# One graph layer and its gate, two blocks merged into one pipelined stage

## What is computed

```python
# layer 0, graph: U = eigenvectors of the normalised Laplacian of adj (64 x 64)
agg = einsum('mn,bnd->bmd', U.T, layernorm(x));  h = relu(agg @ W1 + b1)
x = x + einsum('nm,bmd->bnd', U, h @ W2 + b2)
# layer 0, experts: gate, the best 2 of 8, softmax over these two
z = layernorm(x);  logits = z @ Wg + bg;  top_w, top_i = top_k(logits, 2);  w = softmax(top_w)
x = x + sum over the two experts of w * (gelu(z @ W1[e] + b1[e]) @ W2[e] + b2[e])
# layer 1, graph (two mixings with adj, then LSTMs over windows of nodes), layer 1, experts (best 1 of 8)
```

## Time and profile before

| what | us |
|---|---|
| median of three runs | 1786.4 (1785.47 to 1787.1) |
| the profiled execution | 1787.28, its span 1785.5 |
| busy: PE / DVE / ACT / POOL | 1275.3 / 836.7 / 761.6 / 602.5 |
| first matmul of `layer_gnn0` | at 336.69 |
| first normalize of `gate0` | at 392.66 |
| first DVE instruction of `route` | at 443.90 |

### The profile page before, as it was taken

How to read it: one execution, slowest core, us unless ns; L and a number is a source line. 1 busy time by engine, 2 the same in 40 slices (tenths; PEclk the granted TensorE clock), 3 DMA queues, 4 the chain that set the end, 5 groups by cost and what they waited for, 6 DMA issues and landing times. The chain is left out here.

```text
span 1785.5 us, 26992 instructions
## 1 busy us (share of the span) xinstructions
PE 1275.3 (71%) x6055; PEld 905.0 (51%) x6056; DVE 836.7 (47%) x3364; ACT 761.6 (43%) x1937; POOL 602.5 (34%) x1091
## 2 busy tenths in 40 slices
PE   2444225577679999966777779989885995799900
PEld 1233225467569999963434433444333453799900
DVE  5777999575842222225565523333336336311122
ACT  3555445111555555433344335444445553555400
POOL 4666145000035566547555200000000000355466
PEclk9999656685789999996688779999997997699955
DMA  9200000002002222221111000000000110122333
GB/s 261 63 1 1 1 1 1 1 24 71 0 25 70 71 71 71 66 56 52 37 37 34 20 1 0 0 0 0 0 0 0 42 47 6 24 69 70 61 94 100
DMA packets 87134, 69.13 MB, mean 39 GB/s; under 512 B 11158, under 2 KB 77020, under 8 KB 87068
## 3 DMA queue, kind: packets, MB, share of 16 engines
q1 hardware_dynamic: 73884, 41.40, 8.1%
q0 software_dynamic: 13184, 27.03, 6.3%
HBM read 41.38 MB, written 27.00 MB: 38 GB/s over the span
## 5 line engine op out<-in xcount | busy, mean ns | idle before, releaser
L1250 POOL COPY g_idx<-sitter 128x1 int32 (+1 forms) x78 | 11.9, 179 | 553.7 <-POOLq L1112 538.1
L1657 PE MATMUL ps<-BIG,w_ihT 128*128 x364 | 162.2, 589 | 20.7 <-ACT e_go L1679 15.0
L1304 ACT ACTIVATE c_H<-ps,c_b 128x256 f32<-128x256 f32 x284 | 117.4, 471 | 131.4 <-PE ps L1333 130.6
L1254 POOL DMA_INDIRECT c_Z<-z,c_idx x142 | 138.6, 976 | 81.0 <-POOLq L1252 57.4
L1444 POOL DMA_INDIRECT d_Y<-y,seat x128 | 129.1, 1009 | 94.5 <-DVE X L1458 49.1
L1346 PE MATMUL ps<-w_dn,c_H 128*128 x1136 | 139.0, 276 | 2.1 <-ACT c_H L1304 2.0
L1333 PE MATMUL ps<-c_ZT,c_w 128*128 128x256 f32 x568 | 136.3, 383 | 1.2 <-ACT c_ZT L1292 1.2
L1346 PEld LDWEIGHTS ps<-w_dn,c_H 128*128 128x128 f32 x1136 | 132.4, 192 | 3.5 <-issue 3.0
L1657 PEld LDWEIGHTS ps<-BIG,w_ihT 128*128 128x128 f32 x364 | 69.3, 194 | 108.6 <-issue 108.6
L1663 PE MATMUL ps<-e_hs,w_hhT 128*128 128x512 f32 (+1 forms) x256 | 110.8, 575 | 12.9 <-DVE e_hs L1709 12.9
L1333 PEld LDWEIGHTS ps<-c_ZT,c_w 128*128 128x128 f32 x568 | 103.6, 192 | 13.4 <-ACT c_ZT L1292 2.0
(11 more groups left out here) (495 smaller groups left out, 2951.8 us busy)
## 6 DMA issues: line engine op xcount, KB each, us to landing
y<-c_ys SPq DMA_DIRECT2D x71, 128.0 KB, 1.8
z<-ZB SPq DMA_DIRECT2D x32, 256.0 KB, 2.2
y<-g_ys SPq DMA_DIRECT2D x39, 128.0 KB, 1.8
out_dram<-X SPq DMA_DIRECT2D x32, 128.0 KB, 1.9
c_Z<-z,c_idx POOLq DMA_INDIRECT x142, 2.5
w_up<-in_L_ffn_W_dram SPq DMA_DIRECT2D x1, 2048.0 KB
w_dn<-in_L_ffn_W_dram SPq DMA_DIRECT2D x8, 256.0 KB
w_dn<-in_L_ffn_Wd_dram SPq DMA_DIRECT2D x8, 256.0 KB
```

Of the source, the lines that this page charges most:

```text
L1250: pool.tensor_copy(idx[h][u][:, :], k.sitter[:, ds(t * HALVES + h, 1)]).then_inc(copied, 1)
L1254: pool.indirect_dma_start(Z[u][:, h, :], None, z, bass.IndirectOffsetOnAxis(ap=idx[h][u][:, 0:1], axis=0)).then_inc(fetched[u], 16)
L1304: act.activation(H[u][:, c, :], UP[u][c // 2][:, c % 2 * SLOT_TILE:(c % 2 + 1) * SLOT_TILE], ACT.Gelu, bias=(b1[u] if w_up is not None els ...
L1657: last = pe.matmul(o, k.w_ihT[:, w, :], state(i, u, s, p, wide, lanes), start=True, stop=(s == 0))
```

## The change

`layer_gnn0` and `gate0` are replaced by one block, `layer0`. Turns 0 to 27 run on all engines; the gate's work on group n is done in turn n + 9 (`LAG`).

- The layer's MIX and BACK, and the gate's transposes, have one PSUM bank each instead of two; DN keeps two. DVE's order in a turn is add(g-2), stats(g-3), bias(g-1), and then the chunk work below.
- Mean and 1/std are formed per chunk of four groups (16 tiles): `variance` in turns 6, 10, 14, 18 and `scale` in turns 7, 11, 15, 19, with a Sqrt of ACT between.
- Normalising moves from DVE to POOL (two tiles of a group) and ACT (the other two).
- The gate's scores use the strips of `gate1`: four matmuls of 128 x 32 weights and 128 moving columns, a copy by ACT (`sc`), and one matmul with the identity for all four tiles.
- The picks run per chunk, in DVE turns 15, 19, 23 and 27.
- The softmax's Exp moves to ACT's part of `route`, and its three DVE instructions to the start of `gnn1`.
- One more memset on POOL at the kernel's start, since the gate's weight tile is now 32 columns wide.

```diff
-CONSTS = 11 + E
+CONSTS = 12 + E
...
+                      pool.memset(k.upper[:, :], 0.0), pool.memset(k.w_gate1[:, :, :], 0.0),
+                      pool.memset(k.w_gate0[:, :], 0.0)]
...
-def layer_gnn0(nc, k, sem):
...
-def gate0(nc, k, sem, z):
...
+def layer0(nc, k, sem, z):
+    mixed, h_ready, dn_done, o_ready, back_done, added, s_stats = (
+        sem("a_" + n) for n in "mixed h dn o back added stats".split())
+    s_va, s_root, scaled, z_act, z_pool, turned, turned_sb, scores, scores_sb, logits = (
+        sem("b_" + n) for n in "va root scaled z_act z_pool turned turned_sb scores scores_sb logits".split())
     kept = [sem(f"b_kept{u}") for u in range(2)]
+    MIX, DN, BACK, TR, SC, GA = k.ps[0], k.ps[1:3], k.ps[3], k.ps[4], k.ps[5], k.ps[6:8]
+    CHUNK = 4
+    WIDE = CHUNK * GT
+    LAG = 2 * CHUNK + 1
+    TURNS = GROUPS + LAG + 3
+    zt = rows_of_tiles(z)
     with ExitStack() as own:
+        def mine(name, shape):
+            return own.enter_context(nc.sbuf_tensor(f"a_{name}", shape, F32))
+        O, HT = ([mine(f"{n}{u}", [P, GC]) for u in range(2)] for n in ("O", "H"))
+        sc = [mine(f"sc{u}", [P, P]) for u in range(2)]
+        nbias, m1, m2 = (mine(n, [P, TILES]) for n in ("nbias", "m1", "m2"))
+        tm = mine("tm", [P, WIDE, E])
         block = own.enter_context(nc.Block())
+        def chunk(q):
+            return slice(q * WIDE, (q + 1) * WIDE)
         @block.vector
         def _(dve):
             link = Chain(dve, k.ch)
+            def add_bias(g):
+                dve.wait_ge(dn_done, g + 1)
+                if g >= 2:
+                    dve.wait_ge(back_done, g - 1)
+                dve.tensor_tensor(O[g % 2][:, :].rearrange("p (t d) -> p t d", d=D),
+                                  DN[g % 2][:, :].rearrange("p (t d) -> p t d", d=D),
+                                  k.b_g0dn[:, None, :].to_broadcast([P, GT, D]), ALU.add).then_inc(o_ready, 1)
+            def add_back_tokens(g):
+                dve.wait_ge(back_done, g + 1)
+                dve.tensor_tensor(group_of(k.X, g), group_of(k.X, g),
+                                  BACK[:, :].rearrange("p (t d) -> p t d", d=D), ALU.add).then_inc(added, 1)
+            def variance(q):
+                r = chunk(q)
+                me, ve, mo, vo = (k.st6[:, r, n] for n in (1, 2, 4, 5))
+                dve.wait_ge(s_stats, (q + 1) * CHUNK)
+                got = link.put(dve.tensor_tensor(k.va[:, r], me, mo, ALU.subtract))
+                link.put(dve.tensor_tensor(k.vb[:, r], ve, vo, ALU.add))
+                sums = link.put(dve.tensor_tensor(k.mean[:, r], me, mo, ALU.add))
+                link.need(got)
+                link.put(dve.tensor_tensor(k.va[:, r], k.va[:, r], k.va[:, r], ALU.mult))
+                link.need(sums)
+                link.put(dve.tensor_scalar(k.vb[:, r], k.vb[:, r], 1.0 / D, EPS, ALU.mult, ALU.add))
+                link(dve.tensor_scalar(k.mean[:, r], k.mean[:, r], 0.5, None, ALU.mult))
+                dve.scalar_tensor_tensor(out=k.va[:, r], in0=k.va[:, r], scalar=0.25, in1=k.vb[:, r],
+                                         op0=ALU.mult, op1=ALU.add).then_inc(s_va, 1)
+            def scale(q):
+                r = chunk(q)
+                dve.wait_ge(s_root, q + 1)
+                link(dve.reciprocal(k.vb[:, r], k.rstd[:, r]))
+                link(dve.tensor_tensor(k.vb[:, r], k.vb[:, r], k.va[:, r], ALU.mult))
+                link(dve.tensor_tensor(k.vb[:, r], k.vb[:, r], k.rstd[:, r], ALU.add))
+                link(dve.tensor_scalar(k.vb[:, r], k.vb[:, r], 0.5, None, ALU.mult))
+                link(dve.reciprocal(k.rstd[:, r], k.vb[:, r]))
+                dve.scalar_tensor_tensor(out=nbias[:, r], in0=k.mean[:, r], scalar=-1.0, in1=k.rstd[:, r],
+                                         op0=ALU.mult, op1=ALU.mult).then_inc(scaled, 1)
+            def picks(q):
+                r = chunk(q)
+                dve.wait_ge(logits, (q + 1) * CHUNK)
+                link(dve.tensor_tensor(k.LG[:, r, :], GA[q % 2][:, 0:WIDE * E].rearrange("p (t e) -> p t e", e=E),
+                                       k.b_gate0[:, None, :].to_broadcast([P, WIDE, E]), ALU.add))
+                pick_first(dve, link, k, k.LG[:, r, :], WIDE, k.K1[:, r, :], m1[:, r], tm[:, :, :])
+                link(dve.scalar_tensor_tensor(out=k.LG[:, r, :], in0=k.K1[:, r, :], scalar=-1e30, in1=k.LG[:, r, :],
+                                              op0=ALU.mult, op1=ALU.add))
+                pick_first(dve, link, k, k.LG[:, r, :], WIDE, k.K2[:, r, :], m2[:, r], tm[:, :, :])
+                link(dve.tensor_tensor(k.W2[:, r], m2[:, r], m1[:, r], ALU.subtract))
+            for g in range(TURNS + 2):
+                if 2 <= g < GROUPS + 2:
+                    add_back_tokens(g - 2)
+                if 3 <= g < GROUPS + 3:
+                    dve.wait_ge(added, g - 2)
+                    token_stats(dve, k, g - 3, s_stats)
+                if 1 <= g < GROUPS + 1:
+                    add_bias(g - 1)
+                for q in range(GROUPS // CHUNK):
+                    if g == (q + 1) * CHUNK + 2:
+                        variance(q)
+                    if g == (q + 1) * CHUNK + 3:
+                        scale(q)
+                    if g == (q + 1) * CHUNK + LAG + 2:
+                        picks(q)
             link.reset()
+        @block.gpsimd
+        def _(pool):
+            for n in range(GROUPS):
+                u = n % 2
+                pool.wait_ge(scaled, n // CHUNK + 1)
+                if n >= 2:
+                    pool.wait_ge(turned, n - 1)
+                    pool.wait_ge(kept[u], 16 * (n // 2))
+                for j in range(GT // 2):
+                    t = n * GT + j
+                    last = pool.tensor_scalar(k.ZB[u][:, j * P:(j + 1) * P], k.X[:, t, :], k.mean[:, t:t + 1],
+                                              k.rstd[:, t:t + 1], ALU.subtract, ALU.mult)
+                last.then_inc(z_pool, 1)
         @block.scalar
         def _(act):
+            def normalized(n):
+                u = n % 2
+                act.wait_ge(scaled, n // CHUNK + 1)
+                if n >= 2:
+                    act.wait_ge(turned, n - 1)
+                    act.wait_ge(kept[u], 16 * (n // 2))
+                for j in range(GT // 2, GT):
+                    t = n * GT + j
+                    last = act.activation(k.ZB[u][:, j * P:(j + 1) * P], k.X[:, t, :], ACT.Identity,
+                                          bias=nbias[:, t:t + 1], scale=k.rstd[:, t:t + 1])
+                last.then_inc(z_act, 1)
+            for g in range(TURNS):
+                n = g - LAG
+                for q in range(GROUPS // CHUNK):
+                    if g == (q + 1) * CHUNK + 3:
+                        act.wait_ge(s_va, q + 1)
+                        act.activation(k.rstd[:, chunk(q)], k.va[:, chunk(q)], ACT.Sqrt).then_inc(s_root, 1)
+                if g < GROUPS:
+                    act.wait_ge(mixed, g + 1)
+                    if g >= 2:
+                        act.wait_ge(dn_done, g - 1)
+                    act.activation(HT[g % 2][:, :], MIX[:, :], ACT.Relu, bias=k.b_g0up[:, :]).then_inc(h_ready, 1)
+                if 0 <= n < GROUPS:
+                    act.wait_ge(turned, n + 1)
+                    if n >= 2:
+                        act.wait_ge(scores, n - 1)
+                    act.activation(k.ZS[n % 2][:, :], TR[:, :], ACT.Copy).then_inc(turned_sb, 1)
+                if 1 <= n <= GROUPS:
+                    act.wait_ge(scores, n)
+                    if n >= 3:
+                        act.wait_ge(logits, n - 2)
+                    act.activation(sc[(n - 1) % 2][:, :], SC[:, 0:P], ACT.Copy).then_inc(scores_sb, 1)
+                if 0 <= n + 1 < GROUPS:
+                    normalized(n + 1)
         @block.tensor
         def _(pe):
+            for g in range(TURNS):
+                n = g - LAG
+                if g < GROUPS:
+                    if g >= 1:
+                        pe.wait_ge(h_ready, g)
                     for j in range(GT):
                         c = slice(j * P, (j + 1) * P)
+                        last = pe.matmul(MIX[:, c], k.BIG[:, g * GC + j * P:g * GC + (j + 1) * P], k.BDU[:, :],
+                                         start=True, stop=True)
+                    last.then_inc(mixed, 1)
+                if 2 <= g < GROUPS + 2:
+                    pe.wait_ge(o_ready, g - 1)
+                    if g >= 3:
+                        pe.wait_ge(added, g - 2)
+                    pe.matmul(BACK[:, :], k.BDUT[:, :], O[g % 2][:, :], start=True, stop=True).then_inc(back_done, 1)
+                if 0 <= n < GROUPS:
+                    pe.wait_ge(z_act, n + 1)
+                    pe.wait_ge(z_pool, n + 1)
+                    if n >= 1:
+                        pe.wait_ge(turned_sb, n)
+                    for j in range(GT):
+                        c = slice(j * P, (j + 1) * P)
```

(68 more changed lines are left out.)

108 lines of the change are left out of this document (removed).

## The result

Over 6 runs each the changed kernel takes 1778.8 us in the median (1775.7 to 1782.2), the kernel before 1786.75 (1785.5 to 1791.5): ratio 0.995, 95% interval 0.9933 to 0.9968. The forecast was 1774.2 with a range of 1767 to 1782. The profiled execution took 1782.2 (span 1780.4), 5.1 less than the profiled one of before, so the traces have to explain 5.1 us, the medians 8.

The account below looks back on a forecast made before the run. PE's wasteful half-clock gate work and some 18 us holding one engine only bound the stage; turns, stall, gate and tail summed to `route` 12.2 us earlier, so 1787.3 gives 1775.1, 1774.2 as median; range 1767 to 1782.

Parts of the forecast that it names:

- The layer's turn: Layer turns before the gate joins: a closed loop on in-order DVE of 3.35 us, against 2.80 before.
- Mixed turns: Turns 10 to 15, layer and gate together: PE's own sum of 3.9 us each at full clock.
- slower rival: PE's clock does not hold in the layer's turns, at 84% busy: 34 us more, 1808; chance 0.06.
- The stall: DVE turn 15: `scale(2)` and `picks(0)` delay BACK(15) to 401.3, with some 4.5 us of idle PE.
- The gate alone: Groups 8 to 15 after the layer: a chain through single banks and ACT, 2.9 us a group at half clock.
- first rival: Gate alone near 2.45 us a group, through a higher clock or cheaper `picks(0)`: 3 to 5 us less, 1770; chance 0.15.
- Scale(3) ends some 8 us after BACK(15), before ACT needs it: Gate alone: the last chunk's scales come in time, as ACT needs them in its fourth turn, over 10 us.
- The tail: From the last transposes at 423.4 through the last picks of 4.1 us to the start of `route` at 431.7.
- No overlap, the last rival: Some wait puts the gate behind the layer after all: 109 us for the stage, about 1788; chance 0.02.
- The softmax at nothing: Moved softmax costs nothing: ACT's idle 22.14 us in `route` and DVE's 6.61 us wait in `gnn1` cover it.
- second rival: DVE and POOL block each other while POOL normalises: 5 us more, 1779; chance 0.12.
- The total: Whole kernel: `route` begins 12.2 us earlier, taking the profiled 1787.3 to 1775.1, or 1774.2 for the median.

Follow-up runs that it names:

- e_stats_last: Changed kernel with DVE's bias ahead of the statistics in each turn: stage 93.4 us, ratio 0.9923 to the kernel before.
- e_choose_late: Changed kernel with the first chunk's choosing (twelve operations of its picks) moved to turn 20: stage 88.9 us, ratio 0.9911 to the kernel before.
- e_scale_first: Changed kernel with the chunks' scales ahead of the picks within a turn: stage 94.1 us, one time of 1816.7 us.
- e_lag17: Changed kernel with the gate's work lagging 17 turns instead of 9: stage 108.1 us, ratio 1.002 to the kernel before.
- e_pad: Changed kernel with 17 dummy DVE operations at the end of the merged stage: stage 108.0 us, ratio 1.0006 to the kernel before.
- e_again: Changed kernel run again on other cores, no edit: stage 96.1 us, median 1818.3 us, ratio 0.9958 to the kernel before.
- e_before_again: The kernel before run again on other cores, no edit: stage 106.4 us, median 1824.0 us.
- e_old_scores: Changed kernel with scores computed as in the kernel before, without strips, `sc` copy and identity matmul: stage 94.4 us, ratio 0.9919.
- e_three: Changed kernel with bias before statistics, scales ahead of picks and the first chunk's choosing in turn 20: stage 85.9 us, ratio 0.9907.

## Why the prediction was right, point by point

The mechanisms of the stage held, one by one, but that its sum fits to 0.1 us is in part luck. Up to BACK(15) the stage gained 1.1 us on the forecast, the gate alone lost 0.7 of it and the tail 0.3.

- **The layer's turn**: forecast 3.35, measured 3.28, and `e_stats_last` shows that DVE's loop is the cause. Turn 10's BACK was put at 370.75 and came at 370.44. Chunk work in turns 6 and 7 cost nothing, as forecast: the seven turns are 3.27 or 3.28.
- **Mixed turns**: forecast 3.9, measured 3.86 for the row above. Its parts by starts are transposes 0.53 (forecast 0.45), strips 0.36 (0.45) and identity matmul 0.14 (0.2). The reading that strips run beside each other holds at 128 columns: in series at the rate of the earlier trace rows they would be 0.89. The clock held at 1.00 in the layer's turns, which the slower rival had denied. PE's share there is 91% as the stretches count it (23.79 of 26 us). The rival's 84% was worked out from starts and set beside the 78 and 81% of the earlier trace rows, which are counted the other way.
- **The stall**: BACK(15) forecast at 401.3, came at 400.81. The picks took 4.09 (forecast 4.1), 0.32 from start to start, `scale(2)` 1.3 (1.4), and PE was idle 4.21 (4.5). I had `scale(2)` ahead of `picks(0)` in that turn; the code has it behind. The sum is the same there, and it is why the next point failed.
- **The gate alone**: forecast 2.9, measured 2.86, at half clock. The first rival's mechanism, a clock that stays up, shows only with the stall gone (`e_choose_late`), and then for three periods. The argument against the slower rival, that at half clock PE has no gaps and so the clock should rise again, doesn't fit: there PE is busy 39.73 of 40.00 us and the clock stays at 0.50. The step that failed is "Scale(3) ends some 8 us after BACK(15), before ACT needs it": it ended 12.5 us after (413.31), behind `picks(1)`, and cost 1.0 us, shown by `e_scale_first`.
- **The tail**: last transposes forecast 423.4, measured 423.63; `route` forecast 431.7, came at 432.22, so the tail took 8.6 us instead of 8.3. The later start (0.6), the late group 12 and the tail ate what start, turns and stall had given.
- **No overlap, the last rival**: its sum of 109 us for the stage is near what `e_lag17` measured, 108.1, where the gate does stand behind the layer.
- **The softmax at nothing**: held. ACT's table load starts with `route` and hides; from `r_zero` to the first `above` it takes 20.6 us (before 20.5), and the slower loop behind it isn't the Exp's, as `e_pad` shows. `gnn1` as a whole is level.
- **DVE and POOL**: the second rival is refuted. In the changed kernel, `picks(1)` beside POOL's normalising:

```profile
407.93 1.67 POOL L937 TENSOR_SCALAR ZB<-X,mean,rstd 128x128 f32<-128x128 f32 x2 [2.46 <-DMA z<-ZB]
408.44 0.29 DVE L804 TENSOR_TENSOR a_tm<-LG,a_m 128x128 f32<-128x128 f32 x1
408.76 0.34 DVE L805 TENSOR_TENSOR a_tm<-a_tm,prio 128x128 f32<-128x128 f32 x1
```

Two-input operations take 0.29 and 0.34 us inside one POOL stretch of 1.67, where the same two POOL operations took 1.57 in other turns. So they cost each other at most 0.05 and 0.1 us here; over all traces of the experiments a few DVE operations took up to 0.46 beside POOL, and a POOL operation up to 0.94 instead of 0.79. The Trainium skill ("SBUF — State Buffer", Who interferes with whom) says that a DVE instruction with two SBUF inputs contends with a GpSimd instruction that reads SBUF, the later one blocking fully; the trace does not agree for this pair of kinds. For another pair it does. The operation of 1.42 us in the earlier trace rows began 0.02 us after a POOL `tensor_tensor` of 1.39 us (229.59 to 230.98) and ended 0.05 us after it, so the prediction was right not to carry its price over to POOL's `tensor_scalar`.

- **The total**: the stage gave 12.3 us (forecast 12.2), the median 8.0. The step that carried one into the other, that everything outside the stage keeps its length, was the weak one. The profiled execution lost 6.6 us behind it, 3.4 of them in the LSTM stage and 2.5 in the second experts' block, both with a lower granted clock over the same work, and 0.7 in `route`. The median of this kernel lies 4.6 above the forecast, still inside the range. About 1 us in `route` and up to 0.6 ahead of the first MIX come with the change, by the traces; `e_pad` doesn't rule out more. How much of the 4.6 is this, and how much the spread of the later stages between executions (the rest took 1372.9 to 1383.5 us over the eleven traces of the experiments), stays open. Most of a larger gain did arrive: over the eight traces with a shorter stage, `e_again` among them, the median (in one a single time) fell by 1.6 us less on average than the stage did beside `e_before_again`, from 4.6 less in `e_again` to 1.6 more in `e_old_scores`; in `e_three` it was 19.2 for 20.5.

## What to carry to other kernels

When blocks are joined, look on each in-order engine for the loop that one missing buffer closes. Its length is the sum of what stands in it, and an instruction that isn't part of the dependence (here the statistics) can often be moved out of it for nothing. Bulk work per chunk belongs behind the last step that another engine waits for: here 4 us of picking stopped PE, and without the stop the clock stayed up longer, which was worth another 2.8 us. A kernel that is padded back to its old length isn't the old kernel in all else: look at the stages behind the padding before the equal time is read as no cost. And a stage's gain is sure only in that stage: in a kernel whose clock moves between two levels, leave room for some us in the stages behind it.

## What the hardware showed that I had not expected

- Eight passes over 128-column tiles in four column strips take 0.36 us at full clock and 0.59 in the gate alone at half clock, so the strips work side by side even when a pass is this short.
- A stop of 4.21 us on PE was followed by half clock for all eight gate groups, at 2.86 us each but one, against 2.27. Without the stop (`e_choose_late`) two periods were 2.27 and a third 2.60; then the clock fell all the same.
- One extra matmul a turn with no purpose shortened the gate's part of the stage by 1.9 us: the granted clock is 1.00 from 395 to 415, and without the matmul it fell at 403 (0.51 from there to 418).
- An unchanged loop in `route` took 2.75 us for eight items in most changed kernels and 2.64 in the kernel before and the padded one, at a granted clock of 1.00 in both. What sets its rate stays open.
- The kernel before kept TensorE at 0.50 for the 40 us of the gate's loop, though PE was busy 39.73 of them.
